# One program block instead of two, and the first gate product ahead of the last value products

## The chip, the cores and the metric

The kernel runs on one core of a Trainium2 chip. The metric is the device time of one launch in microseconds (us); less is better. The core has five engines that run their own programs and meet at semaphores: TensorE (PE in the profile), VectorE (DVE), ScalarE (ACT), GpSimd (POOL) and SyncE (SP), which here issues nearly all DMA transfers.

## The reference, cut to what matters

A pre-norm transformer layer over x of 4 batches, 512 tokens, width 512, in fp32. Attention has 32 query heads in 8 key/value groups (4 heads share a group, head width 16), rotary positions and a causal mask; the feed-forward width is 1376.

```python
x = x + attn(layernorm(x), Wq, Wk, Wv, Wo)    # softmax(mask(q k^T / 4)) v, then @ Wo
x = x + ffn(layernorm(x), Wg, Wu, Wd)         # (silu(x Wg^T) * (x Wu^T)) @ Wd^T
```

## The kernel before

There are two stages, `phase_1` and `phase_2`, and each opens a block of programs of its own, one program for each engine. At the end of a block all engines meet at a barrier and jump; then the next block begins. Tiles and PSUM banks of the first stage are given back at its end, and those of the second lie over them.

**Stage one, attention.** A batch is an iteration of 32 slots: 8 groups `g` with 4 slots `i` each. In a slot TensorE makes transposed scores of group n (`scores_t`, tile `ps_t`), the scores of group n+2 that give the row maximum (`scores`, `ps_s`), and pieces of dense work: the projections of the next batch, and in the last iteration the output projection of batch 0. ScalarE takes the exponential of `ps_t` into `probs`, GpSimd zeroes what the causal mask forbids (`mask_probs`, semaphore `probs_masked`), and TensorE multiplies `probs` with the values (`weighted_v`, tile `ps_o`, four chunks c of 512, 384, 256 and 128 columns). Chunks 0 and 1 of a group run in its own last slot, chunks 2 and 3 in the second slot of the next group. There is one `ps_o`: chunk 0 of a group waits until the group before it has been copied out (`o_evacuated`). That copy is ScalarE's, except for groups in the table `LAST_O` of the last iteration, which VectorE copies (`last_output`). The copy is stored to DRAM by SP.

The rotated queries and keys are split into parts: GpSimd makes a remainder (`rest_op`), ScalarE copies the high bits in the slots of `LO_SLOT` (`rotated_top`, tile `r_top`), and SP stores the parts one slot later (`store_rotated`). In the next slot with i = 0 SP loads the rows of a later group (`stage_rows`), and with i = 1 the transposed maximum (`stage_max`, `q_rows<-m_t`), which the next group's scores wait for. SP works its list in order.

In the last iteration the second stage's first operands are made too: xt of batch 0 from the transposed x (`last_xt`, VectorE, slots of `LAST_XT`: a cast to `xt_hi`, and the difference `xt_lo`), and the first three tiles of the gate and up weights (`split_ffn`). With these, TensorE has all that the first products of stage two read.

**Stage two, feed-forward.** For each batch, f runs over 11 tiles of the width. TensorE makes the gate and the up product (12 matmuls of 512 columns each, in four PSUM banks used in turn), for f from 3 to 6 the output projection of the next batch (`project_out`), and the down product of tile f-1 (12 matmuls into `ps_y`). Weights are fp32 as two parts: SP loads the raw tile (`load_ffn`), ScalarE casts it to the high part (`split_ffn_hi`), VectorE subtracts (`split_ffn_lo`). In the first batch ScalarE's program begins with the high parts of the down weights 0 and 1, and only then follows the first silu:

```python
            split_ffn_hi(0)
            split_ffn_hi(1)
            iteration(0, True)
```

SP's program of stage two begins with down tile 0, waits until the last group's output has landed in DRAM (`last_o_stored`), loads the last batch's softmax sums, then down tiles 1 and 2, the attention output for the next batch's first projection, and the weights of tile 3, 4 and so on:

```python
            load_ffn(0)
            sp.wait_ge(to.last_o_stored, DMA)
            sp.dma_start(sums, row_sums(d, B - 1)).then_inc(sums_loaded, DMA)
            load_ffn(1)
            load_ffn(2)
```

In iteration f of the first batch ScalarE and VectorE split tile f+2 before they scale and split the attention output (`scale_ctx`, `ctx_high`, `ctx_low`) that the projection at f+1 reads.

Of the kernel before, what the change touches and what calls it, by code (L numbers as in the profile page):

```python
# [1 line left out]

# [3 lines left out]
F32 = mybir.dt.float32  # L6
# [3 lines left out]
ALU = mybir.AluOpType  # L10
# [80 lines left out]
LO_SLOT = {7: 0, 13: 1, 16: 2, 23: 3, 27: 4}  # L91
# [3 lines left out]
LAST_O = {26: 5, 30: 6}  # L95
# [42 lines left out]
def rope_step(b, s):  # L138

    return PRE_STEPS + (KEY_STEPS + 2 * PAIR_STEPS) * (b - 1) + s + 1  # L140

# [117 lines left out]
def phase_1(nc, d, to):  # L259
    with ExitStack() as ctx:  # L260
# [6 lines left out]
        def sem(name):  # L267
            return ctx.enter_context(nc.semaphore(name))
# [91 lines left out]
        ffn_hi_ready = sem("first_ffn_hi_ready")  # L360
        sums_loaded = sem("sums_loaded")
# [50 lines left out]
        block = ctx.enter_context(nc.Block())  # L412


        @block.sync
        def _(sp):
# [146 lines left out]
        @block.gpsimd  # L563
        def _(pool):
# [155 lines left out]
        @block.scalar  # L720
        def _(act):
# [98 lines left out]
            def iteration(b, has_next):  # L820
                done = pieces_at(UNITS_IN[b])[1]
                for slot in range(TT * NKV):
# [4 lines left out]
                    if i == PV_EVACUATE and n >= 1 and (has_next or slot not in LAST_O):  # L827
# [53 lines left out]
        @block.vector  # L881
        def _(dve):
# [72 lines left out]
            def split_ffn(c):  # L955

                dve.wait_ge(ffn_hi_ready, c + 1)
                nc.vector.tensor_tensor(w_lo[:, c], w_lo[:, c].bitcast(F32), w_hi[:, c].bitcast(F32), ALU.subtract)
# [151 lines left out]
        @block.tensor  # L1110
        def _(pe):
# [114 lines left out]
            def weighted_v(b, g, c):  # L1226
                n = NKV * b + g
                pe.wait_ge(probs_masked, TT * n + c + 1)
                if c == 0:
                    if positive(n):  # L1230
                        pe.wait_ge(o_evacuated, n)
                    if g == 0:
                        pe.wait_ge(v_ready, b + 1)
                for j in range(GROUP):
                    mm = nc.tensor.matmul(ps_o[32 * j:32 * j + 2 * DH, P * c:T], v_ones[:, c, g % NKV, :],  # L1235
                                          probs[:, g % 2, j, CHUNK_AT[c]:CHUNK_AT[c + 1]],
                                          start=(c == 0), stop=(c == TT - 1))
                if c == TT - 1:
                    mm.then_inc(pv_done, 1)

            def iteration(b, has_next):
                pieces = pieces_at(UNITS_IN[b])[0]
                for slot in range(TT * NKV):
                    g, i = slot // TT, slot % TT
                    n = NKV * b + g
                    for j in range(GROUP):
# [3 lines left out]
                        if (i, j) in PV_AT:  # L1250
                            after, chunks = PV_AT[i, j]
                            for c in chunks if n + after >= 0 else ():
                                weighted_v(b, g + after, c)
# [32 lines left out]


# [21 lines left out]
def phase_2(nc, d, to):  # L1309
    with ExitStack() as ctx:  # L1310
# [3 lines left out]
        def sem(name):  # L1314
            return ctx.enter_context(nc.semaphore(name))
# [57 lines left out]
        block = ctx.enter_context(nc.Block())  # L1373

        @block.sync
        def _(sp):
# [40 lines left out]

            load_ffn(0)
# [21 lines left out]
        @block.gpsimd  # L1440
        def _(pool):
# [3 lines left out]
        @block.scalar  # L1445
        def _(act):
# [40 lines left out]

            split_ffn_hi(0)
# [6 lines left out]
        @block.vector  # L1495
        def _(dve):
# [74 lines left out]
        @block.tensor  # L1571
        def _(pe):
# [48 lines left out]
            def down(b, f):  # L1621
# [4 lines left out]
                if f == 0 and (not isinstance(b, int) or b > 0):  # L1626
# [8 lines left out]
            def iteration(b, has_next):  # L1635
# [4 lines left out]
                for f in range(FT):  # L1640
# [3 lines left out]
                    for name, weights, ready in (("gate", gate_weights, gate_ready), ("up", up_weights, up_ready)):  # L1644
# [3 lines left out]
                                       lambda q, c: xt[q][:, c, :], KC).then_inc(ready, 1)  # L1648
                    if has_next and 0 <= f - WO_SLOT < TT:
# [7 lines left out]

            iteration(0, True)
# [3 lines left out]


def build(nc, d):
# [51 lines left out]
```

## Time and profile before

| | |
|---|---|
| three runs | 770.94, 773.19, 773.08 us; median 773.08 |
| the profiled execution | 772.49 us, its span 770.8 us, 1.69 us around it |
| PE busy | 737.8 us, 96% of the span |
| DVE, ACT, POOL busy | 445.2, 333.8 and 241.9 us |
| granted TensorE clock | 0.989 of full speed |
| stage one | from 0 to 369.6 us of the span |
| stage two | from 369.6 us to the end |

The profile is of one execution. "Busy" adds up instructions of an engine; a time in brackets is what the engine stood idle ahead of an instruction, and the arrow names what ended it. Where the engine named had long been done, something else ended the wait.

### The profile page before, as it was taken

What the parts mean: (1) busy time and instruction counts of PE and PEld (TensorE: products, weight loads), DVE (VectorE), ACT (ScalarE), POOL (GpSimd) and SP (SyncE); (2) the same over time, 40 slices, a digit from 0 to 9 for tenths busy, and PEclk for the clock granted to TensorE, in tenths of its full rate; (3) what the DMA queues carried; (4) which work ended last, traced back from release to release, by engine and by line L of the source; (5) the groups of instructions that cost most, each with busy time, mean ns of one, the idle gap of its engine ahead of it and who ended that gap; (6) DMA issues with size and microseconds to landing.
All of it is one profiled execution on the core that took longest, in us unless ns stands there. A gap on an engine that the chain in (4) does not pass through costs nothing.

```text
span 770.8 us, 12186 instructions
## 1 busy us (share of the span) xinstructions
PE 737.8 (96%) x4149; PEld 502.4 (65%) x4164; DVE 445.2 (58%) x1136; ACT 333.8 (43%) x646; POOL 241.9 (31%) x467
## 2 busy tenths in 40 slices
PE   5889999999999999998999999999999999999998
PEld 4645444554444543443788888888888888788886
DVE  6897789888987889997355443234232333231212
ACT  4337678767976778667343222111121111111111
POOL 4257885688658774556000000000000000000000
PEclk9869999999999999999999999999999999999999
DMA  7337587234434455530592103211014020030001
GB/s 272 98 108 250 182 280 239 67 87 125 119 96 130 142 179 151 160 99 29 174 310 72 42 14 118 88 59 51 14 48 142 27 82 27 0 110 1 1 0 55
DMA packets 74759, 81.86 MB, mean 106 GB/s; under 512 B 8864, under 2 KB 58528, under 8 KB 74496
## 3 DMA queue, kind: packets, MB, share of 16 engines
q1 hardware_dynamic: 73408, 79.98, 32.7%
q10 hardware_dynamic: 1296, 1.18, 0.5%
q8 instruction: 30, 0.49, 0.3%
q14 instruction: 25, 0.20, 0.1%
HBM read 57.02 MB, written 33.36 MB: 117 GB/s over the span
## 4 chain that ended last, share of the span: by engine, by line
PE 51%; DVE 0%; issue 0%; DVEq 0%
PE bank L1578 35%; PE ps_y L1630 15%; PE bank L1617 1%; DVE x_in L1560 0%; DVEq L1559 0%
## 5 line engine op out<-in xcount | busy, mean ns | idle before, releaser
L929 DVE CUSTOM_DVE_ANT_0 ps_s<-ps_s,mask_row 128x512 f32<-128x512 f32 (+1 forms) x360 | 192.1, 583 | 36.6 <-PE ps_s L1188 34.0
L792 ACT ACTIVATE probs<-ps_t 128x512 f32<-128x512 f32 (+1 forms) x352 | 178.2, 560 | 68.6 <-PE ps_t L1222 68.3
L1535 DVE TENSOR_TENSOR h<-h,bank 128x512 f32<-128x512 f32 (+1 forms) x44 | 30.2, 687 | 212.8 <-PE bank L1578 211.6
L1188 PE MATMUL ps_s<-k_rows,q_rows 96*128 96x256 bf16 (+3 forms) x512 | 141.0, 309 | 5.7 <-DVE m_raw L929 2.9
L1222 PE MATMUL ps_t<-q_rows,k_rows 98*128 98x512 bf16 (+1 forms) x352 | 126.9, 364 | 4.4 <-DMA q_rows<-m_t 2.4
L240 POOL TENSOR_TENSOR var_eps<-mean_var,eps 128x1 f32<-128x1 f32 x16 | 3.0, 189 | 281.7 <-DVE mean_var L235 281.7
L1473 ACT ACTIVATE h<-bank 128x512 f32<-128x512 f32 (+1 forms) x44 | 26.3, 597 | 145.2 <-PE bank L1578 145.2
L1235 PE MATMUL ps_o<-probs,v_ones 128*32 128x512 f32 (+3 forms) x1024 | 82.0, 438 | 3.4 <-POOL probs L693 1.1
L693 POOL TENSOR_SCALAR_AFFINE_SELECT probs<-probs 128x512 f32<-128x512 f32 x128 | 83.4, 652 | 0.0
L1479 ACT CAST h_hi<-h 128x512 fp32r<-128x512 f32 (+1 forms) x44 | 27.3, 620 | 126.5 <-DVE h L1535 126.5
L1188 PEld LDWEIGHTS ps_s<-k_rows,q_rows 96*128 96x128 bf16 x512 | 48.2, 100 | 47.8 <-DVE m_raw L929 22.3
L1630 PE MATMUL ps_y<-wd_hi,h_hi 128*128 128x512 f32 (+1 forms) x176 | 68.8, 391 | 0.0
L1222 PEld LDWEIGHTS ps_t<-q_rows,k_rows 98*128 98x128 bf16 x352 | 34.2, 98 | 53.1 <-issue 18.3
L1630 PE MATMUL ps_y<-wd_lo,h_hi 128*128 128x512 f32 (+1 forms) x176 | 68.5, 389 | 0.0
L1630 PE MATMUL ps_y<-wd_hi,h_lo 128*128 128x512 f32 (+1 forms) x176 | 68.5, 389 | 0.0
L1235 PEld LDWEIGHTS ps_o<-probs,v_ones 128*32 128x32 f32 x1024 | 27.2, 109 | 43.3 <-issue 30.4
L691 POOL TENSOR_TENSOR carrier<-half 128x1 f32<-128x1 f32 x128 | 26.8, 209 | 89.9 <-ACT probs L792 89.8
L929 DVE DVE_READ_ACCUMULATOR2_ANT m_raw<- 128x1 f32 x360 | 50.3, 140 | 0.0
L1578 PE MATMUL bank<-xt_hi,wg_hi 128*128 128x512 f32 (+1 forms) x128 | 50.0, 390 | 0.0
L1578 PE MATMUL bank<-xt_hi,wg_lo 128*128 128x512 f32 (+1 forms) x128 | 49.9, 390 | 0.0
L1578 PE MATMUL bank<-xt_hi,wu_lo 128*128 128x512 f32 (+1 forms) x128 | 49.9, 390 | 0.0
L1578 PE MATMUL bank<-xt_lo,wu_hi 128*128 128x512 f32 (+1 forms) x128 | 49.9, 390 | 0.0
(167 smaller groups left out, 1366.1 us busy)
## 6 DMA issues: line engine op xcount, KB each, us to landing
scratch_o<-o_sb SPq DMA_DIRECT2D x31, 256.0 KB, 2.4
q_rows<-scratch_q_parts SPq DMA_DIRECT2D x32, 192.0 KB
x_in<-in_x SPq DMA_DIRECT2D x16, 256.0 KB, 4.0
q_rows<-scratch_q_parts SPq DMA_DIRECT2D x32, 128.0 KB
o_in<-scratch_o SPq DMA_DIRECT2D x64, 64.0 KB
inverse<-scratch_inverse SPq DMA_DIRECT2D x64, 64.0 KB
x_res<-in_x SPq DMA_DIRECT2D x16, 256.0 KB, 2.7
out<-x_in SPq DMA_DIRECT2D x16, 256.0 KB, 2.1
```

Source lines behind the costliest of these rows:

```text
L691: nc.gpsimd.tensor_tensor(carrier[:, g % 2, c:c + 1], half[:, 0:1], half[:, 0:1], ALU.add)
L693: nc.gpsimd.affine_select(out=diagonal, in_=diagonal, compare_op=ALU.is_ge, fill=0.0, base=0, pattern=[[0, GROUP], [1, P]], channel_multip ...
L792: nc.scalar.activation(probs[:, g % 2, heads * u:heads * (u + 1), CHUNK_AT[c]:CHUNK_AT[c + 1]], ps_t[:, pos % S_BANKS, 0:heads * CHUNK_N[c ...
L929: taken = nc.vector.tensor_tensor_reduce(out=head, in0=head, in1=mask_row[:, T - width:T], scale=1.0, scalar=LOWEST, op0=ALU.add, op1=ALU. ...
L1188: mm = nc.tensor.matmul(bank[:, place], q_rows[r][0:ROWS, j, P * q:P * (q + 1)], k_rows[r][0:ROWS, 0:width], start=(place == 0), stop=(mas ...
L1222: nc.tensor.matmul(ps_t[:, pos % S_BANKS, 0:heads * width], k_rows[r][:, P * c:P * (c + 1)], q_rows[r][:, heads * u:heads * (u + 1), P * c:T],
L1235: mm = nc.tensor.matmul(ps_o[32 * j:32 * j + 2 * DH, P * c:T], v_ones[:, c, g % NKV, :], probs[:, g % 2, j, CHUNK_AT[c]:CHUNK_AT[c + 1]], ...
L1473: nc.scalar.activation(h[0:m, r], bank[units["gate", f] % BANKS][0:m, :], ACT.Silu).then_inc(silu_done, 1)
L1479: nc.scalar.copy(h_parts[0][0:m, r], h[0:m, r]).then_inc(h_hi_ready, 1)
L1535: nc.vector.tensor_tensor(h[0:m, r], h[0:m, r], bank[units["up", f] % BANKS][0:m, :], ALU.mult).then_inc(h_ready, 1)
L1578: mm = nc.tensor.matmul(out, weights(w, c), moving(m, c), start=(c == 0 and n == 0), stop=(c == chunks - 1 and n == 2))
L1630: mm = nc.tensor.matmul(ps_y[:, t], h_parts[w][0:m, r, P * t:P * (t + 1)], wd[p][0:m, f, :], start=(f == 0 and k == 0), stop=(f == FT - 1 ...
```

## The change

Four things are done.

1. The two stages return their programs instead of opening blocks, and one block calls the first and then the second. The barrier between them is gone. In its place single waits stand: SP and ScalarE wait for the copy of the last group's output (`handed_over`) at the start of stage two, TensorE waits for it ahead of its first down product, and ahead of its first gate product it waits for `xt_lo` and for the split gate weights (`first_tiles_ready`).
2. TensorE makes the first gate product before chunks 2 and 3 of the last group's value products (`last_values`).
3. `LAST_O` moves VectorE's copy of group 6 of the last batch from slot 30 to slot 29, ahead of the third `last_xt`.
4. `LO_SLOT` moves three of the five copies of high bits of each batch ahead: from slots 16, 23 and 27 to 14, 22 and 26.

```diff
-LO_SLOT = {7: 0, 13: 1, 16: 2, 23: 3, 27: 4}
+LO_SLOT = {7: 0, 13: 1, 14: 2, 22: 3, 26: 4}
-LAST_O = {26: 5, 30: 6}
+LAST_O = {26: 5, 29: 6}
...
-                if not has_next:
-                    for c in (2, 3):
-                        weighted_v(b, NKV - 1, c)
-
...
+        def last_values(pe):
+
+            for c in (2, 3):
+                weighted_v(pe, B - 1, NKV - 1, c)
...
+        def handed_over(engine):
+
+            engine.wait_ge(o_evacuated, GROUPS)
+
+        def first_tiles_ready(pe):
+
+            pe.wait_ge(dense_evacuated, LAST_UNIT0 + TT + KC)
+            pe.wait_ge(ffn_split, KC)
...
+            attention.handed_over(sp)
             load_ffn(0)
             sp.wait_ge(to.last_o_stored, DMA)
...
+            attention.handed_over(act)
             split_ffn_hi(0)
             split_ffn_hi(1)
...
-                if f == 0 and (not isinstance(b, int) or b > 0):
+                if f == 0 and isinstance(b, int) and b == 0:
+                    attention.handed_over(pe)
+                elif f == 0:
                     pe.wait_ge(y_evacuated, TT * b)
...
+                        if first and (name, f) == ("gate", 0):
+                            attention.last_values(pe)
...
+            attention.first_tiles_ready(pe)
             iteration(0, True)
...
-        phase_1(nc, d, handover)
-        phase_2(nc, d, handover)
+        attention = phase_1(nc, d, handover, ctx)
+        feed_forward = phase_2(nc, d, handover, ctx, attention)
+        block = ctx.enter_context(nc.Block())
...
+        @block.tensor
+        def _(pe):
+            attention.tensor(pe)
+            feed_forward.tensor(pe)
```

TensorE between the stages, before: the value products of the last group, the two jumps, and the first gate product (`bank`). The names in brackets are the semaphores that an instruction waits for.

```order
L1235 MATMUL ps_o<-probs,v_ones 32x384 x3
L1235 MATMUL ps_o<-probs,v_ones 32x256 [waits probs_masked]
L1235 MATMUL ps_o<-probs,v_ones 32x256 x3
L1235 MATMUL ps_o<-probs,v_ones 32x128 [waits probs_masked]
L1235 MATMUL ps_o<-probs,v_ones 32x128 x3
L260 UNCONDITIONAL_BRANCH
L1571 UNCONDITIONAL_BRANCH [waits barrier_Pool_Activation_PE_DVE_SP_release]
L1578 MATMUL bank<-xt_hi,w_hi 128x512
```

The same place now, from the last chunk-1 product to the first of the up product; of the twelve matmuls of the gate product the first and the last two are shown.

```order
L1132 MATMUL ps_o<-probs,v_ones 32x384 x3
L1600 MATMUL bank<-xt_hi,w_hi 128x512 [waits first_ffn_split,dense_evacuated]
...
L1600 MATMUL bank<-xt_lo,w_hi 128x512
L1600 MATMUL bank<-xt_hi,w_lo 128x512
L1132 MATMUL ps_o<-probs,v_ones 32x256 [waits probs_masked]
L1132 MATMUL ps_o<-probs,v_ones 32x256 x3
L1132 MATMUL ps_o<-probs,v_ones 32x128 [waits probs_masked]
L1132 MATMUL ps_o<-probs,v_ones 32x128 x3
L1600 MATMUL bank<-xt_hi,w_hi 128x512
```

The eight matmuls of chunks 2 and 3 now stand behind the gate product, and with them everything that waits for the last group's output.

VectorE's last work of stage one, before: `COPY o_sb` is group 6, `COPY o_in` group 7, each `CAST` with the `TENSOR_TENSOR` behind it one `last_xt`.

```order
L958 TENSOR_TENSOR w_lo<-w_lo,w_hi 128x768 [waits first_ffn_hi_ready]
L979 CAST xt_hi<-ps_s 128x512 [waits dense_ready]
L901 TENSOR_TENSOR xt_lo<-ps_s,xt_hi 128x512 [waits xt_hi_ready]
L986 COPY o_sb<-ps_o 128x512 [waits o_stored0,pv_done]
L979 CAST xt_hi<-ps_s 128x512 [waits dense_ready]
L901 TENSOR_TENSOR xt_lo<-ps_s,xt_hi 128x512 [waits xt_hi_ready]
L986 COPY o_in<-ps_o 128x512 [waits pv_done]
```

And now.

```order
L970 TENSOR_TENSOR w_lo<-w_lo,w_hi 128x768 [waits first_ffn_hi_ready]
L999 COPY o_sb<-ps_o 128x512 [waits o_stored0,pv_done]
L992 CAST xt_hi<-ps_s 128x512 [waits dense_ready]
L913 TENSOR_TENSOR xt_lo<-ps_s,xt_hi 128x512 [waits xt_hi_ready]
L992 CAST xt_hi<-ps_s 128x512 [waits dense_ready]
L913 TENSOR_TENSOR xt_lo<-ps_s,xt_hi 128x512 [waits xt_hi_ready]
L999 COPY o_in<-ps_o 128x512 [waits pv_done]
```

Group 6's copy stands ahead of two `last_xt` instead of one.

SP in a batch of stage one around slots 14 to 17, before: `r_top` and `r_low` are `store_rotated`, `k_rows` and `q_rows<-scratch_q_parts` are `stage_rows`, `q_rows<-m_t` is `stage_max`.

```order
L434 DMA scratch_wu_raw<-in_wu 16x11008 x2
L452 DMA k_rows<-scratch_k_parts 48x1x512
L455 DMA q_rows<-scratch_q_parts 48x4x512
L452 DMA k_rows<-scratch_k_parts 32x1x512
L455 DMA q_rows<-scratch_q_parts 32x4x512
L452 DMA k_rows<-scratch_k_parts 16x512
L455 DMA q_rows<-scratch_q_parts 16x4x512
L409 DMA scratch_q_parts<-r_top 16x8x512 x2
L409 DMA scratch_q_parts<-r_low 16x8x512
L465 DMA q_rows<-m_t 2x16x128
```

And now.

```order
L449 DMA scratch_wu_raw<-in_wu 16x11008
L426 DMA scratch_q_parts<-r_top 16x8x512 x2
L426 DMA scratch_q_parts<-r_low 16x8x512
L449 DMA scratch_wu_raw<-in_wu 16x11008
L467 DMA k_rows<-scratch_k_parts 48x1x512
L470 DMA q_rows<-scratch_q_parts 48x4x512
L467 DMA k_rows<-scratch_k_parts 32x1x512
L470 DMA q_rows<-scratch_q_parts 32x4x512
L467 DMA k_rows<-scratch_k_parts 16x512
L470 DMA q_rows<-scratch_q_parts 16x4x512
L480 DMA q_rows<-m_t 2x16x128
```

The three stores moved ahead of the six row loads; ahead of `q_rows<-m_t` stand the same transfers as before.

## Rows read from the trace of the kernel before

**Rows 1.** Waits of TensorE from 369 to 771 us: total, times, longest.

```profile
PE bank L1578 <- PEq L260: 1.9, 1, 1.9
```

**Rows 2.** Timeline of TensorE between the stages: start, duration, instruction, idle before.

```profile
361.69 0.62 PE L1235 MATMUL ps_o<-probs,v_ones 128*32 128x256 f32 x12
...
363.88 0.38 PE L1222 MATMUL ps_t<-q_rows,k_rows 98*128 98x512 bf16 x1
365.38 2.36 PE L1235 MATMUL ps_o<-probs,v_ones 128*32 128x512 f32 x32 [1.11 <-POOL probs L693]
369.60 0.47 PE L1578 MATMUL bank<-xt_hi,w_hi 128*128 128x512 f32 x1 [1.86 <-PEq L260]
```

**Rows 3.** Timeline of VectorE there.

```profile
361.31 0.95 DVE L958 TENSOR_TENSOR w_lo<-w_lo,w_hi 128x768 fp32r<-128x768 f32 x1
...
363.94 0.69 DVE L901 TENSOR_TENSOR xt_lo<-ps_s,xt_hi 128x512 fp32r<-128x512 f32 x1
364.55 0.68 DVE L986 COPY o_sb<-ps_o 128x512 f32<-128x512 f32 x1
365.14 0.68 DVE L979 CAST xt_hi<-ps_s 128x512 fp32r<-128x512 f32 x1
365.86 0.69 DVE L901 TENSOR_TENSOR xt_lo<-ps_s,xt_hi 128x512 fp32r<-128x512 f32 x1
367.79 0.69 DVE L986 COPY o_in<-ps_o 128x512 f32<-128x512 f32 x1 [1.24 <-PE ps_o L1235]
```

**Rows 4.** Timeline of GpSimd there: the mask of chunk 1.

```profile
363.70 0.63 POOL L693 TENSOR_SCALAR_AFFINE_SELECT probs<-probs 128x512 f32<-128x512 f32 x1
```

**Rows 5.** Timeline of SP's queue behind the last copy.

```profile
368.51 0.33 SPq L471 DMA_DIRECT2D scratch_o<-o_in  x1
...
370.50 0.62 SPq L1420 DMA_DIRECT2D x_res<-scratch_o  x1
371.18 1.05 SPq L1393 DMA_DIRECT2D wd_lo<-scratch_wd_raw  x2
```

**Rows 6.** Timelines of ScalarE, VectorE and TensorE: down tile 1 to the first down product.

```profile
374.00 0.62 ACT L1452 CAST wd_hi<-wd_lo 128x512 fp32r<-128x512 f32 x1 [1.30 <-DMA wd_lo<-scratch_wd_raw]
374.63 1.28 ACT L1473 ACT_TABLE_LOAD   x1
...
377.94 0.69 DVE L1540 TENSOR_TENSOR h_lo<-h,h_hi 128x512 fp32r<-128x512 f32 x1 [0.69 <-ACT h_hi L1479]
...
380.57 0.39 PE L1630 MATMUL ps_y<-wd_hi,h_hi 128*128 128x512 f32 x1
```

**Rows 7.** The same engines and SP: weight tile 4 to the first projection.

```profile
387.13 0.51 SPq L1393 DMA_DIRECT2D wd_lo<-scratch_wd_raw  x1
...
391.65 0.62 ACT L1451 CAST wg_hi<-wg_lo 128x512 fp32r<-128x512 f32 x1 [1.31 <-DMA wd_lo<-scratch_wd_raw]
...
395.49 0.69 DVE L218 TENSOR_TENSOR ctx_lo<-o_in,ctx_hi 128x512 fp32r<-128x512 f32 x1 [0.69 <-ACT ctx_hi L213]
...
396.89 0.39 PE L1578 MATMUL bank<-wo_hi,ctx_hi 128*128 128x512 f32 x1
```

**Rows 8.** Stage one: SP's stores and maximum at slot 17, and TensorE's wait.

```profile
100.28 1.22 SPq L409 DMA_DIRECT2D scratch_q_parts<-r_top  x2
...
102.94 0.68 SPq L465 DMA_DIRECT2D q_rows<-m_t  x1
...
106.10 0.39 PE L1222 MATMUL ps_t<-q_rows,k_rows 98*128 98x512 bf16 x1 [0.66 <-DMA q_rows<-m_t]
```

**Rows 9.** TensorE's longest wait after its start, and clock by stretch: us, busy (instructions), clock, DMA share, GB/s.

```profile
33.58 1.12 PE L1149 MATMUL ps_t<-ident,v_t 128*128 128x128 f32 x4 [2.64 <-ACT v_t L759]
...
33.00:36.00 3.00, 1.74 (x7) 0.55 0.28 88
...
42.00:45.00 3.00, 3.00 (x14) 0.50 0.49 130
...
364.00:370.00 6.00, 3.03 (x36) 1.00 0.22 86
```

More of the change, by code:

```diff
@@ L1 @@
 from contextlib import ExitStack
+from dataclasses import dataclass
+from typing import Callable
 import concourse.bass as bass
@@ L140, in rope_step @@
     return PRE_STEPS + (KEY_STEPS + 2 * PAIR_STEPS) * (b - 1) + s + 1
+@dataclass
+class Programs:
+    sync: Callable
+    gpsimd: Callable
+    scalar: Callable
+    vector: Callable
+    tensor: Callable
+    last_values: Callable = None
+    handed_over: Callable = None
+    first_tiles_ready: Callable = None
 class Handover:
@@ L267, in sem @@
         def sem(name):
[L268 removed]
+            return sems.enter_context(nc.semaphore(name))
         ident = to.ident
@@ L826, in iteration @@
                         max_evacuate(n + 1)
-                    if i == PV_EVACUATE and n >= 1 and (has_next or slot not in LAST_O):
+                    if i == PV_EVACUATE and n >= 1 and (has_next or g - 1 not in LAST_O.values()):
                         o_evacuate(b, g - 1)
@@ L1107, in _, with weighted_v, tensor_engine @@
             last_output(NKV - 1)
-        @block.tensor
-        def _(pe):
+        def weighted_v(pe, b, g, c):
+            n = NKV * b + g
+            pe.wait_ge(probs_masked, TT * n + c + 1)
+            if c == 0:
+                if positive(n):
+                    pe.wait_ge(o_evacuated, n)
+                if g == 0:
+                    pe.wait_ge(v_ready, b + 1)
+            for j in range(GROUP):
+                mm = nc.tensor.matmul(ps_o[32 * j:32 * j + 2 * DH, P * c:T], v_ones[:, c, g % NKV, :],
+                                      probs[:, g % 2, j, CHUNK_AT[c]:CHUNK_AT[c + 1]],
+                                      start=(c == 0), stop=(c == TT - 1))
+            if c == TT - 1:
+                mm.then_inc(pv_done, 1)
+        def last_values(pe):
+            for c in (2, 3):
+                weighted_v(pe, B - 1, NKV - 1, c)
+        def tensor_engine(pe):
             PRODUCTS = ((0, 0), (0, 1), (1, 0))
@@ L1224, in scores_t @@
                                  start=True, stop=True).then_inc(scores_t_ready, 1)
[L1226 to L1239, printed above, removed]
             def iteration(b, has_next):
@@ L1252, in iteration @@
                             for c in chunks if n + after >= 0 else ():
-                                weighted_v(b, g + after, c)
+                                weighted_v(pe, b, g + after, c)
                         for place, kind, k, piece in pieces.get((slot, j), ()):
@@ L1306, with phase_2 @@
 RING_LAST = ring_units(False)
-def phase_2(nc, d, to):
+def phase_2(nc, d, to, sems, attention):
     with ExitStack() as ctx:
@@ L1666, in build, with _ @@
         handover = Handover(nc, ctx)
-        phase_1(nc, d, handover)
-        phase_2(nc, d, handover)
+        attention = phase_1(nc, d, handover, ctx)
+        feed_forward = phase_2(nc, d, handover, ctx, attention)
+        block = ctx.enter_context(nc.Block())
+        @block.sync
+        def _(sp):
+            attention.sync(sp)
+            feed_forward.sync(sp)
+        @block.gpsimd
+        def _(pool):
+            attention.gpsimd(pool)
+            feed_forward.gpsimd(pool)
+        @block.scalar
+        def _(act):
+            attention.scalar(act)
+            feed_forward.scalar(act)
+        @block.vector
+        def _(dve):
+            attention.vector(dve)
+            feed_forward.vector(dve)
+        @block.tensor
+        def _(pe):
+            attention.tensor(pe)
+            feed_forward.tensor(pe)
 def rope_tables():
```

40 lines of the change are left out of this document (17 added, 23 removed).

## The prediction

> **What bounds the kernel now.** I read the page's busy times first: TensorE is busy for 96% of the span. Then its waits by stretch. In stage two the view has a single entry [rows 1], the wait that ends at 369.60: once started, TensorE runs to the end with no wait on another engine, so an operand that comes earlier brings nothing there, and one that comes later than TensorE needs it costs its full lateness. Time can only be won ahead of 369.60. The timeline there [rows 2] has two holes. After the last transposed scores (363.88) the value products start at 365.38, after 1.11 us idle, and after they end (365.38 + 2.36 = 367.74) the first gate product starts at 369.60, after 1.86 us.
>
> Who ends them? The first is put down to GpSimd's mask, but the mask of chunk 1 was done at 363.70 + 0.63 = 364.33 [rows 4], and that of chunk 0 before it. The other condition of chunk 0 is group 6's copy, which VectorE ended at 364.55 + 0.68 = 365.23 [rows 3], about 0.1 before the products. So the copy was the wait. It could have run earlier: its value products ended at 361.69 + 0.62 = 362.31 [rows 2] and VectorE's weight split at 361.31 + 0.95 = 362.26 [rows 3]. The second hole is the last copy (367.79 to 368.48), SP's store and the barrier. The gate product itself needs none of this: `xt_lo` was done at 365.86 + 0.69 = 366.55 [rows 3].
>
> **The change, part by part: TensorE up to the up product.** With the copy at 362.4, chunks 0 and 1 can start behind the last scores, at about 364.2. How long do they take? Matmuls of 1280 columns in all four chunks took 2.36 us, so the 896 columns of the first two take 1.65 and the other two 0.7, to which I give 0.15 for the changes of shape: until 365.85, and 0.85. On VectorE the last cast moves into the slot that the copy held, 364.55, and the last difference follows 365.86 - 365.14 = 0.72 later, at 365.27, and ends at 365.96. The gate product therefore starts at 366.1, held by `xt_lo` by some 0.2. It takes 12 steps of (380.57 - 369.60)/48 = 0.2285 us [rows 2, 6], 2.74, and with 0.1 at its start the values of chunks 2 and 3 begin at 368.95 and end at 369.8; their masks were ready by 366.2. The up product starts at 369.75. Before it started at 369.60 + 2.74 = 372.35. **TensorE is 2.6 us ahead here.** The barrier and the jumps are part of the 1.86 us, and what replaces them is covered by the gate product.
>
> **What hangs on the last value products.** The same move makes the last group's output later in absolute time: copy at 369.85 instead of 367.79, **2.06 us later**. Behind that copy stands SP's whole list: store at 370.57 (368.51 before), sums load when the store has landed, 370.50 - 368.51 = 1.99 later, at 372.56, and only then down tile 1, at 373.24 (371.18) [rows 5]. The 0.7 us saved between the store and down tile 0 by the missing barrier does not help, since the list waits for the store. ScalarE casts tile 1 ahead of its first silu, so it starts at 374.00 + 2.06 = 376.06 [rows 6]; table load, silu, product, cast and difference follow as before, and `h_lo` is done at 377.94 + 0.69 + 2.06 = 380.69. TensorE wants it at 369.75 + 36 steps = 377.95. **It waits 2.8 us and starts the down product at 380.75, against 380.57 before.** The lead is gone, and 0.2 more. The cover that hid this chain was 380.57 - 378.63 = 1.94 us; 2.06 later and 2.6 sooner needed is more than it has.
>
> I weigh one rule here. On this chain the row has the table load at 1.28 us, with the silu 0.02 behind it [rows 6]. The Trainium skill (ScalarE: Activation LUTs, What ACT_TABLE_LOAD costs) gives about 1.28 us and a drain of 1.38 on top; the trace has the first and shows no drain. By the page `h_lo` would come 1.4 later and the total below would be +1.6 instead of +1.45; the measured row decides.
>
> What is late next? SP issued from 370.50 to beyond 387.13 without a wait that showed, so the later transfers shift by 2.06 too. Weight tile 4 (last issue 387.13) is what ScalarE waited for at 391.65; from there the splits and the scaling run one after another to `ctx_lo`, done at 395.49 + 0.69 = 396.18 [rows 7]. TensorE started the projection at 396.89: cover 0.7. Now `ctx_lo` is done at 398.24 and TensorE, by then 0.2 late, arrives at 397.07. **It waits another 1.25 us and starts at 398.33, 1.45 after its old time.** The tiles behind have more room: their steps on TensorE are 10.9 us apart and ScalarE waited for no further tile in the trace. The rest of the kernel keeps the 1.45.
>
> **Stage one.** The copies of high bits are moved, not added. ScalarE does the same 1.05 us in a slot where the next exponential is needed by TensorE two products later; I cost it at nothing, with 0.3 as bound for each of three places in three batches where it might not be covered, 0.9 at most if a third of them miss. The gain would be in the waits for `q_rows<-m_t`, such as 0.66 at 106.10. But SP is the queue in front of it, issuing back to back (stores 100.28, maximum 102.94) [rows 8], and the stores stand ahead of the maximum now as before, so it goes out at the same time. Bounds from below: all four such waits, 2.4 us in total. I take 0, being nearest to the queue's order, and keep -0.7 to +0.9. Six row loads go out 1.9 us later at slot 16 (100.2 to 102.0), and are read at 105.6; the maximum, issued later still at 102.94, landed by 106.1, so they just make it.
>
> **Sum.** -2.6 + 2.8 + 1.25 = +1.45 us, on the profiled execution's own 772.49 us: 773.9, which I give as 774.0 with a little for stage one. The median of the three runs is 0.6 above the profiled execution, so against it this is a change of 0.1 to 0.2%, inside the 0.3% (2.3 us) that a measurement of this kernel tells from no change.
>
> **Rivals.**
> - *No late tile* (16%). If down tile 1 lands so much sooner that `h_lo` is ready at 378, and tile 4 likewise, the 2.6 us stay: 769.9, faster. For it: in the old trace the two loads were issued 1.6 us apart beside the sums, now down tile 0 is out of the way longer. Against: tile 1 took 374.00 - 371.18 = 2.8 us, and the store alone 1.99, so nearly three would have to vanish.
> - *Only the first wait* (12%). If tile 4 isn't 2 us later, since SP's list has slack I don't see, the sum is +0.2: 772.7, no change.
> - *The clock falls* (15%). This one ends slower. After a wait of 2.64 us at 33.58 the granted clock was 0.55 in the next stretch and still 0.50 at 42 to 45, that is 1.2 GHz; with 1.11 and 1.86 us idle at 364 to 370 it stayed 1.00 [rows 9]. A wait of 2.8 us is of the first kind. At half clock each us costs 0.5; the first 1.25 us lost are free, as they only fill the second wait. So the total is 0.2 + L for a loss L above 1.25, and the kernel is slower by 0.3% once the low clock lasts over 4.2 us; up to 12 us would be 778.7, and 7 us, between, 776.2. Against: TensorE is dense from there on, which it wasn't at 33. The Trainium skill (TensorE: Matmul & The Clock Gate, What's actually happening) says that the low clock is the default and activity releases it, which leaves both open.
> - *Stage one moves after all* (7%): 1 in 7 of it faster, the others split between no change and slower, 772 to 777.
>
> **How the numbers follow.** The forecast has 50%, with a range of its own of 773.0 to 775.2 (0.9 for stage one, and 0.5 for landing times each way). Faster is the first rival and a bit of the last, 0.17; no change the forecast, the second rival and half of the last, 0.65; slower the clock and the rest, 0.18. The range runs from the first rival's 769.8 to 776.3, which leaves out the longer half of the clock's case and little else.
>
> **What the next profile would show.** Right: no idle ahead of the last group's first value products; the gate product at 366.1 with the values behind it; the last copy at 369.85; SP's sums load 2.0 us behind its store; a wait of about 2.8 us ahead of the first `ps_y` product, on VectorE's `h_lo`, and one of 1.2 ahead of the first `wo` product, on `ctx_lo`; TensorE's total of waits in stage two near 4 us. Wrong: no wait at `ps_y` (first rival), a clock below 1.00 behind 378 (third), or the last scores of stage one more than 1 us away from 363.88 (fourth).

## The result and the profile after

The changed kernel takes 775.74 us (median of 8 executions) against 773.13 for the kernel before; the ratio is 1.0049, with a 95% interval of 1.0033 to 1.0066. So it is slower, by 0.3 to 0.7%. Measured again in a later series it was 775.68 against 772.28, ratio 1.0036 [1.0021, 1.0052]. I had forecast no change (774.0). The ratio is not the quotient of the two medians, which is 1.0034 in the first series and 1.0044 in the second.

The profiled execution was the slowest of the eight, 778.65 us with a span of 776.9. Its busy times are those of before plus 3.7 us of TensorE, on matmuls that are the same in number:

```profile
PE 741.5 (95%) x4149; PEld 503.9 (65%) x4164; DVE 445.1 (57%) x1136; ACT 334.2 (43%) x646; POOL 242.5 (31%) x467
```

More busy time on the same work suggests a lower clock. First the timeline of TensorE between the stages, the counterpart of [rows 2]:

```profile
367.99 0.38 PE L1254 MATMUL ps_t<-q_rows,k_rows 98*128 98x512 bf16 x1
368.30 1.71 PE L1132 MATMUL ps_o<-probs,v_ones 128*32 128x512 f32 x16
370.11 0.50 PE L1600 MATMUL bank<-xt_hi,w_hi 128*128 128x512 f32 x1
...
373.06 0.86 PE L1132 MATMUL ps_o<-probs,v_ones 128*32 128x256 f32 x16
373.85 0.50 PE L1600 MATMUL bank<-xt_hi,w_hi 128*128 128x512 f32 x1
...
384.97 0.47 PE L1654 MATMUL ps_y<-wd_hi,h_hi 128*128 128x512 f32 x1 [2.62 <-issue]
```

The last scores stand 4.11 us later than before (367.99 against 363.88). From there the order does what it says: both holes are gone, the gate product starts 2.12 us behind the scores (5.72 before), the up product at 5.86 (8.47 before). Then comes the wait ahead of the first down product, 2.62 us. The chain that it waits for begins in SP's queue, in its timeline (counterpart of [rows 5]):

```profile
374.70 0.33 SPq L486 DMA_DIRECT2D scratch_o<-o_in  x1
375.36 0.33 SPq L1417 DMA_DIRECT2D wd_lo<-scratch_wd_raw  x1
376.70 0.63 SPq L1445 DMA_DIRECT2D x_res<-scratch_o  x1
377.38 1.06 SPq L1417 DMA_DIRECT2D wd_lo<-scratch_wd_raw  x2
```

and goes on in those of ScalarE and VectorE (counterparts of [rows 6]):

```profile
380.24 0.62 ACT L1475 CAST wd_hi<-wd_lo 128x512 fp32r<-128x512 f32 x1 [1.67 <-DMA wd_lo<-scratch_wd_raw]
380.88 1.28 ACT L1496 ACT_TABLE_LOAD   x1
382.18 0.60 ACT L1496 ACTIVATE h<-bank 128x512 f32<-128x512 f32 x1
...
384.18 0.69 DVE L1563 TENSOR_TENSOR h_lo<-h,h_hi 128x512 fp32r<-128x512 f32 x1 [0.68 <-ACT h_hi L1502]
```

Each row stands 4.13 to 4.18 us behind the time forecast for it (store 370.57, sums 372.56, tile 1 373.24, cast 376.06), which is the lateness of stage one and nothing else: this chain was forecast to a tenth. The table load again took 1.28 us with the silu 0.02 behind it. The Trainium skill (ScalarE: Activation LUTs, What ACT_TABLE_LOAD costs) has a drain on top; this trace doesn't show one either.

What I had only as a rival is the clock behind the wait, here by windows (columns: window, length, busy and instructions, granted clock, DMA share, GB/s):

```profile
382.00:385.00 3.00, 0.38 (x3) 1.00 0.47 119
385.00:388.00 3.00, 3.00 (x9) 0.60 0.74 186
388.00:392.00 4.00, 4.00 (x17) 0.87 0.76 230
```

A mean of 0.60 is the half clock (1.2 GHz, 0.50) for 80% of 3 us, and 0.87 for 26% of 4 us: together 3.4 us, of which half is lost. No wait stands ahead of the first projection. Where do the 4.1 us of stage one come from? Most of it shows in one place. TensorE's timeline has a wait there:

```profile
127.94 0.39 PE L1254 MATMUL ps_t<-q_rows,k_rows 98*128 98x512 bf16 x1 [1.99 <-DMA q_rows<-m_t]
```

and the windows around it show the clock:

```profile
124.00:128.00 4.00, 1.86 (x19) 1.00 0.86 266
128.00:132.00 4.00, 4.00 (x17) 0.70 0.86 289
132.00:136.00 4.00, 3.94 (x36) 0.87 0.25 75
```

Again a wait of 2 us, and half clock behind it. Before, TensorE had no wait here. The wait is for the transposed maximum of slot 25, so I looked at SP's queue, first in the kernel before:

```profile
113.92 1.19 SPq L434 DMA_DIRECT2D scratch_wd_raw<-in_wd  x2
116.41 1.22 SPq L409 DMA_DIRECT2D scratch_q_parts<-r_top  x2
...
118.35 0.77 SPq L452 DMA_DIRECT2D k_rows<-scratch_k_parts  x1
...
121.75 0.67 SPq L465 DMA_DIRECT2D q_rows<-m_t  x1
```

and in the changed one:

```profile
114.89 0.57 SPq L449 DMA_DIRECT2D scratch_wd_raw<-in_wd  x1
116.89 1.22 SPq L426 DMA_DIRECT2D scratch_q_parts<-r_top  x2
...
118.80 1.39 SPq L449 DMA_DIRECT2D scratch_wd_raw<-in_wd  x1
120.24 0.77 SPq L467 DMA_DIRECT2D k_rows<-scratch_k_parts  x1
...
123.62 0.67 SPq L480 DMA_DIRECT2D q_rows<-m_t  x1
```

Before, SP issued two weight copies and then stood idle from 115.11 until the rotated parts were ready at 116.41. Now the stores stand ahead of the second copy: SP waits about as long (1.43 us against 1.30), and the copy, 1.39 us of issue, falls behind the stores. The maximum goes out 1.87 us later, of which 0.95 is the kernel's general lateness by then (110.80 against 109.85 for the maximum before it) and 0.92 is new. That can't be all of a wait of 1.99 us: TensorE now starts 4.32 us behind the issue of the maximum, where before it started 3.32 behind it (at 125.07) without a wait. So the maximum also landed later behind its own issue. What that comes from is taken up behind the experiments on the queue.

### The profile page after: what moved, and what is told of

Its sections match the earlier page's. It is cut to its first block, busy times and chain, and to the rows that moved or that the text cites. A ratio compares the mean times of both kernels' runs of the same rounds, so it can differ in the third digit from the quotient of the medians.

```text
span 776.9 us, 12176 instructions
## 1 busy us (share of the span) xinstructions
PE 741.5 (95%) x4149; PEld 503.9 (65%) x4164; DVE 445.1 (57%) x1136; ACT 334.2 (43%) x646; POOL 242.5 (31%) x467
## 4 chain that ended last, share of the span: by engine, by line
PE 81%; DVE 7%; POOL 4%; ACT 3%; DMA 2%; issue 2%; ACTq 0%; SPq 0%; POOLq 0%; DVEq 0%
PE bank L1600 35%; PE ps_y L1654 15%; PE ps_t L1254 7%; PE ps_o L1132 7%; PE ps_s L1220 6%; PE ps_d L1172 6%; DVE ps_s L941 2%; DMA q_rows<-m_t 2%; ACT probs L805 2%; PE ps_d L1193 1%; POOL rot L609 1%; POOL turned L609 1%; PE bank L1639 1%; POOL rot L613 1%; POOL probs L707 1%
```

## The experiments

"Scores to end" is the time from the start of the last transposed scores to the end of the span; it holds the handover and stage two, and nothing of stage one. Before it was 770.8 - 363.88 = 406.9. Each value is of one profiled execution. All ratios are to the kernel before, executed in turn with it.

**The LO_SLOT table alone** (kernel before, new table).

```diff
-LO_SLOT = {7: 0, 13: 1, 16: 2, 23: 3, 27: 4}
+LO_SLOT = {7: 0, 13: 1, 14: 2, 22: 3, 26: 4}
```

> The kernel before with the changed LO_SLOT alone; the two blocks stay. Two theories. A (two places): in the changed kernel's profile stage one ended 4.1 us later, and its first loss stands at 124 to 128, where SP stores the high bits ahead of a weight copy that used to fill SP's idle time, the transposed maximum is issued 0.9 later than its surroundings, TensorE waits 1.99 us and its clock is below 1.00 for some 10 us. Then this kernel is slower than before by 1 to 4 us, with that wait of 1.5 to 2 us near 127. B (handover only): that was one execution's accident, and this kernel is within 0.5 us of before in the median, with a wait below 0.7 there.

774.58 against 772.57 us, ratio 1.0023 [1.0007, 1.0039]. A wait of 2.24 us at 127.17, with the clock at 0.50 from 130 to 132. So stage one's loss comes with this table alone, and needs nothing of the rest of the change.

**The changed kernel with the old LO_SLOT.**

> The changed kernel with LO_SLOT of before: one block, first gate product ahead of the last value products, earlier copy of group 6. A: stage one as before (the last transposed scores end within 1 us of 363.9), up product 2.6 us earlier than before, a wait of 2.6 us ahead of the first ps_y product, then some 3 us at half clock that cost 1.5 to 2 us, no wait or one under 1.2 ahead of the first projection; in all +1.5 to +2.2 us against before. B: nearly the whole slowdown of the changed kernel, +2.3 to +3 us.

773.71 against 772.57, ratio 1.0015 [0.9999, 1.0030]. The last scores at 363.59, a wait of 2.65 ahead of the down product, the clock 0.50 at 382 to 384, scores to end 408.9: 2.0 more than the profile of before. The median says 1.2. The difference of the two numbers became clear only later (below, the clock).

**All value products ahead of the gate product** (single block kept, old LO_SLOT).

```diff
-                        if first and (name, f) == ("gate", 0):
-                            attention.last_values(pe)
...
+            attention.last_values(pe)
             attention.first_tiles_ready(pe)
             iteration(0, True)
```

> As the one with the old LO_SLOT, but all four chunks of the last value products stand ahead of the gate product; the single block stays. Theory A (the order costs, the barrier was the gain): values end near 366.5, the gate product starts at 366.6 instead of 369.6, the last copy ends near 367.4 (368.48 before), so the chain to h_lo ends near 377.6 and TensorE wants it at 377.6: a wait under 0.3 at ps_y, the clock stays at 1.00; ahead of the first projection a wait of about 1 us, since ctx_lo is only 1.05 earlier. In all -1.5 to -2.5 us against before. Rival C (the gate product ahead is what gains, the masks of chunks 2 and 3 hold TensorE without it): gate product not before 367.5, and a total within 1 us of before.

770.22 against 772.57, ratio 0.9975 [0.9961, 0.9989]: faster than before; scores to end 405.0. TensorE's timeline:

```profile
362.57 0.38 PE L1254 MATMUL ps_t<-q_rows,k_rows 98*128 98x512 bf16 x1
362.88 2.40 PE L1132 MATMUL ps_o<-probs,v_ones 128*32 128x512 f32 x32
365.21 0.50 PE L1600 MATMUL bank<-xt_hi,w_hi 128*128 128x512 f32 x1
...
393.58 0.50 PE L1600 MATMUL bank<-wo_hi,ctx_hi 128*128 128x512 f32 x1 [0.68 <-DVE ctx_lo L233]
```

The masks of chunks 2 and 3 do not hold TensorE: all four chunks run in 2.40 us without a gap. The gate product starts 2.64 us behind the scores, 0.5 later than with the gate product first, and the up product, twelve steps on at 368.06, at 5.49 against 5.86: earlier. Moving the gate product ahead filled no time that was still empty, and it held the last copy back by a whole product. Rival C falls.

**SP issues down tiles 1 and 2 ahead of its wait for the last store** (gate product first, old LO_SLOT).

```diff
             load_ffn(0)
+            load_ffn(1)
+            load_ffn(2)
             sp.wait_ge(to.last_o_stored, DMA)
             sp.dma_start(sums, row_sums(d, B - 1)).then_inc(sums_loaded, DMA)
-            load_ffn(1)
-            load_ffn(2)
```

> As the one with the old LO_SLOT (gate product first), but SP issues down tiles 1 and 2 ahead of its wait for the last store. Theory A: the cast of tile 1 follows that of tile 0 at once, h_lo is 1.6 us earlier, so the wait ahead of ps_y is 1.0 to 1.2 us instead of 2.6 and the clock stays at 1.00; then a wait of 1.5 to 2.9 us ahead of the first projection, as weight tile 4 and what follows it come at most 1.1 earlier; in all +0.3 to +1.5 us against before. If instead the tiles were not what h_lo waits for, the wait at ps_y stays at 2.6 and the time that of the kernel with the old LO_SLOT.

773.38 against 772.57, ratio 1.0006 [0.9994, 1.0018]. TensorE's waits of stage two, in its timeline:

```profile
379.67 0.47 PE L1654 MATMUL ps_y<-wd_hi,h_hi 128*128 128x512 f32 x1 [1.05 <-issue]
398.82 0.50 PE L1600 MATMUL bank<-wo_hi,ctx_hi 128*128 128x512 f32 x1 [2.59 <-DVE ctx_lo L233]
```

and the windows behind the second (the granted clock stands behind the count of instructions):

```profile
398.00:400.00 2.00, 1.18 (x5) 0.93 1.12 363
400.00:402.00 2.00, 2.00 (x6) 0.50 1.13 359
```

The first wait fell from 2.6 to 1.05, as worked out, and the second operand in line took it over: 2.59 us ahead of the projection, and the half clock came there instead. Scores to end is 410.1, 1.2 more than with the old LO_SLOT alone, but this execution was the slowest of its twelve. By the medians the two kernels are alike (773.38 and 773.71). This shows both chains of the forecast, and that mending this one alone gives little or nothing.

**Both repairs**: the tiles ahead, and ctx ahead of the split of tile f+2, on ScalarE and in the same way on VectorE.

```diff
+                    if has_next and 0 <= f - WO_SLOT + 1 < TT:
+                        ctx_hi(b + 1, f - WO_SLOT + 1)
                     if first and f + 2 < FT:
                         split_ffn_hi(f + 2)
-                    if has_next and 0 <= f - WO_SLOT + 1 < TT:
-                        ctx_hi(b + 1, f - WO_SLOT + 1)
```

With the gate product first:

> The same two repairs (tiles ahead of the store's wait, ctx ahead of the split) with the gate product first, as in the changed kernel, and the old LO_SLOT. If tile 4 ahead of ctx was the cause of the 2.6 us ahead of the first projection: that wait is gone, the 1.0 us ahead of ps_y stays (nothing repairs it), the clock stays at 1.00, -1.3 to -1.6 us against before, so 1.5 us behind the values-first kernel with the same repairs. Rival: a wait of over 1 us ahead of the projection stays, and the time is within 0.5 us of before.

771.78 against 773.48, ratio 0.9980 [0.9959, 1.0001]. The wait ahead of the projection is gone, 1.15 us ahead of the down product is left, the clock stays; scores to end 405.6. With the value products first:

> A kernel meant to beat both: old LO_SLOT, one block, all value products ahead of the gate product, SP issues down tiles 1 and 2 ahead of its wait for the last store, and ScalarE and VectorE make the attention output's parts ahead of the split of tile f+2. From the values-first kernel's trace: the gate product starts 3.1 us sooner behind the last scores than before, and its only wait in stage two was 0.7 ahead of the first projection, which the new order of ctx and split should take away. If lateness of ctx_lo came from tile 4 standing ahead of it: no wait of TensorE in stage two over 0.2 us, clock 1.00, -3.0 to -3.3 us against before. Rival: ctx_lo is held by its own loads, and the 0.7 stays; -2.4 us.

769.73 against 773.48, ratio 0.9955 [0.9931, 0.9978]. Stage two has no wait left; scores to end 403.7, 3.2 below before. A second series, beside the changed kernel:

> The kernel with all value products first, down tiles ahead of the store's wait and ctx ahead of the split, once more beside the changed one: no wait in stage two, clock 1.00 there, -2.5 to -3.5 us against before and some 5 to 6 us ahead of the changed kernel.

768.77 against 772.28, ratio 0.9954 [0.9937, 0.9972]. The counterpart of [rows 2], from that profile:

```profile
364.31 0.38 PE L1254 MATMUL ps_t<-q_rows,k_rows 98*128 98x512 bf16 x1
364.62 2.40 PE L1132 MATMUL ps_o<-probs,v_ones 128*32 128x512 f32 x32
366.95 0.50 PE L1600 MATMUL bank<-xt_hi,w_hi 128*128 128x512 f32 x1
...
377.96 0.39 PE L1654 MATMUL ps_y<-wd_hi,h_hi 128*128 128x512 f32 x1
...
394.28 0.39 PE L1600 MATMUL bank<-wo_hi,ctx_hi 128*128 128x512 f32 x1
```

No brackets: nothing stands idle. This version beats both kernels, by 3.5 and 6.9 us.

**The single block alone** (values first, LO_SLOT and LAST_O of before).

> The single block alone: value products ahead of the gate product, LO_SLOT and LAST_O of before. The 1.1 us hole ahead of the last value products is back, and only the barrier's part of the other hole is won, so the gate product starts some 2.0 us sooner behind the last scores than before; the last copy stays where it was, so h_lo and ctx_lo come as late as before. Theory (only as much lead is kept as the tightest operand allows, 0.7 at ctx_lo): waits of under 0.3 at ps_y and about 1.3 ahead of the first projection, -0.5 to -0.9 us in all. Rival (what is won ahead of the gate product stays won): -2.0 us.

771.49 against 773.48, ratio 0.9987 [0.9964, 1.0009], too wide to decide by time. The profile decides: the gate product starts 3.78 behind the scores instead of 5.72, so 1.94 are won there, and scores to end is 406.2, so 0.7 are kept. The rival that all of it stays won falls by this profile; the interval of the ratio (-2.8 to +0.7 us) would still hold it. The wait ahead of the projection was 0.68, not 1.3: TensorE came there 0.4 later than reckoned (31.50 us behind the scores, where 33.01 - 1.94 = 31.07 was), and `ctx_lo` some 0.2 sooner than before.

**The weight copy issued ahead of the stores** (kernel before, new LO_SLOT), in slots 15 and 23 of the first iteration.

```diff
+                    if not positive(b) and slot in (15, 23):
+                        copy_raw(2 * g + i - 2)
                     if has_next and slot - 1 in LO_SLOT:
                         store_rotated(sp, b + 1, LO_SLOT[slot - 1])
...
-                    if not positive(b) and i >= 2 and g < 6:
+                    if not positive(b) and i >= 2 and g < 6 and slot not in (15, 23):
                         copy_raw(2 * g + i - 2)
```

> The kernel before with the changed LO_SLOT, and in slots 15 and 23 of the first iteration the weight copy is issued ahead of the stores, so that it fills SP's wait for them again. Theory A (queue order: the copy of 1.4 us behind the stores delays the maximum): the wait of 2 us near 127 and the half clock behind it are gone (a wait under 0.7 there, clock 1.00), and the time is within 0.7 us of before. Rival (ScalarE's copy of high bits in the earlier slots is what costs): the wait and +1.5 to +2 us stay.

775.22 against 773.48, ratio 1.0022 [1.0006, 1.0039]. The two readings disagree: no wait over 0.35 us from 112 to 135, but the median was as far off as with the table alone. By the time, theory A had fallen; so I took the entries apart. The same profile has the rest of the answer: ahead of two other maxima TensorE waited 1.17 us (at 106.75) and 1.04 us (at 267.7), where before it was 0.66 and nothing.

**Entry 23 to 22 alone**, twice, and **the other two entries alone.**

> The kernel before with one entry of LO_SLOT changed, 23 to 22. Theory A (this entry alone puts the stores ahead of the last weight copy, which delays the maximum near 127): the wait of about 2 us near 127 and the half clock behind it are here, and most of what LO_SLOT costs, +1 to +2 us. Rival: it is shared by the other two entries, +0.5 us or less and a wait under 1 us near 127.

> The kernel before with LO_SLOT 23 changed to 22, a second time. +1 to +3 us whatever the cause; between 124 and 128 a wait of 0.7 to 2.3 us.

> The kernel before with the other two entries changed, 16 to 14 and 27 to 26. Theory A: no wait over 1 us near 127; only the small waits for the maximum near 106 and 269 grow, by 0.4 and 0.5 to 1.0, as in the two profiles with the changed table: +0.3 to +1.2 us. Rival (the weight copy was not the cause, since issuing it first left the time as it was): +1.5 us or more.

Entry 22: 774.61 against 772.28, ratio 1.0033 [1.0016, 1.0049], and 773.67 against 771.90, 1.0016 [1.0001, 1.0030]. The other two: 773.32 against 772.28, 1.0012 [0.9996, 1.0028]. The wait near 126 was 0.71 us in the first profile; TensorE's timeline of the second shows:

```profile
127.00 0.39 PE L1222 MATMUL ps_t<-q_rows,k_rows 98*128 98x512 bf16 x1 [2.12 <-DMA q_rows<-m_t]
```

and its window behind that wait:

```profile
128.00:132.00 4.00, 3.66 (x35) 1.00 0.96 325
```

So the wait varies from one execution to the next, and here no half clock followed it.

**Queue order or ScalarE's copy?** Entry 22 with the weight copy first, and entry 22 for ScalarE only, with SP's stores left in slot 24 by a table of their own:

```diff
-LO_SLOT = {7: 0, 13: 1, 16: 2, 23: 3, 27: 4}
+LO_SLOT = {7: 0, 13: 1, 16: 2, 22: 3, 27: 4}
+STORE_SLOT = {8: 0, 14: 1, 17: 2, 24: 3, 28: 4}
...
-                    if has_next and slot - 1 in LO_SLOT:
-                        store_rotated(sp, b + 1, LO_SLOT[slot - 1])
+                    if has_next and slot in STORE_SLOT:
+                        store_rotated(sp, b + 1, STORE_SLOT[slot])
```

> The kernel before with LO_SLOT 23 changed to 22, and the weight copy of slot 23 issued ahead of the stores. Queue order as the cause: within 0.8 us of before, no wait over 0.5 us between 124 and 128. ScalarE as the cause: +1.5 us or more, as with the entry alone.

> The kernel before with ScalarE's copy of high bits in slot 22 instead of 23, and SP's stores left in slot 24. Queue order as the cause: within 0.8 us of before. ScalarE as the cause: +1.5 us or more.

772.40 against 771.90, ratio 0.9995 [0.9979, 1.0011], and 770.94 against 771.90, 0.9986 [0.9970, 1.0001]. Neither costs anything that shows, and neither profile has a wait of TensorE over 0.7 us between 45 and 280. For this entry ScalarE is cleared, and the queue order is the cause of what it costs; the profiles carry this more than the times, whose intervals still overlap with that of the entry alone (1.0001 to 1.0030).

With the other two entries in, the kernel with the copy first still measured +1.7 us; the two entries alone measured +0.9 with an interval that includes that. The profiles say where it goes. Ahead of the maximum near 106 us TensorE waited 0.99 us on average in the five profiles with these entries (0.78 to 1.17) and 0.53 in the thirteen without them (0.36 to 0.91); ahead of the one near 267 it was 0.83 (0.53 to 1.14) against 0.09 (nothing in ten, 0.74 at most). Together that is 1.2 us. So the other two entries are the likely rest; no run shows what in their place makes these waits.

**The changed kernel, and its version with the old LO_SLOT, once more.**

> The changed kernel once more, unchanged, for a second profile and more executions. If its first profile was typical: waits of about 2 us near 127 and 2.6 us ahead of the first ps_y product, granted clock 0.50 behind both, no wait ahead of the first projection, +2 to +4 us against before. If the stage-one wait was an accident of one execution, it is below 1 us here and the kernel is within 1.5 us of before.

> The changed kernel with the old LO_SLOT, a second time: a wait of 2.6 to 2.8 us ahead of the first ps_y product. Behind it the clock is 0.50 for some 3.4 us (2 of the 3 profiles with this wait so far) or stays at 1.00 (1 of 3), and the stretch from the last scores to the end is 408.9 us with the fall, about 407.5 to 408 without. +0 to +2.3 us against before.

The changed kernel: ratio 1.0036 as above, waits of 1.12 near 125 and 2.79 ahead of the down product, neither followed by a lower clock, as the windows of its second profile show:

```profile
124.00:128.00 4.00, 3.19 (x21) 1.00 0.92 325
...
378.00:382.00 4.00, 1.21 (x6) 1.00 0.52 120
382.00:385.00 3.00, 3.00 (x15) 1.00 0.84 242
```

Its profiled execution took 773.94, the fastest of its series. With the clock up the second wait of the forecast is there in TensorE's timeline, but small:

```profile
398.26 0.50 PE L1600 MATMUL bank<-wo_hi,ctx_hi 128*128 128x512 f32 x1 [0.23 <-DVE ctx_lo L233]
```

The old LO_SLOT: 774.32 against 771.90, ratio 1.0025 [1.0011, 1.0039], a wait of 2.67, half clock behind it, scores to end 408.8.

**How the queue order costs.** This last profile has SP's old order, and it happens to issue the row loads and the maximum just as late as the changed kernel did. From the timelines of SP's queue and of TensorE:

```profile
113.84 1.19 SPq L449 DMA_DIRECT2D scratch_wd_raw<-in_wd  x2
...
119.20 0.77 SPq L467 DMA_DIRECT2D k_rows<-scratch_k_parts  x1
...
122.59 0.68 SPq L480 DMA_DIRECT2D q_rows<-m_t  x1
...
125.14 0.39 PE L1254 MATMUL ps_t<-q_rows,k_rows 98*128 98x512 bf16 x1 [0.23 <-DMA q_rows<-m_t]
```

TensorE was ready at 125.14 - 0.23 = 124.91, so the maximum was issued 2.32 us ahead of that and the first row load 5.71 ahead. In the changed kernel it was 2.33 and 5.71 (ready at 127.94 - 1.99 = 125.95). The issue times are alike, and the waits are 0.23 and 1.99. So the issue of the maximum is not what makes the wait; its landing is. In the five profiles with the stores ahead of the second weight copy TensorE started 3.05 to 4.45 us behind the issue of the maximum. In the thirteen with both copies ahead of the stores it started 2.2 to 3.7 us behind it, with a wait of 0.48 at most, and in five of these the maximum was issued as late as 2.20 to 2.41 us ahead of the need.

What differs is the weight copy, 688 KB, which took 5.1 to 6.6 us from issue to landing by the DMA view (for the pair of copies that is the median). Reckoned with that, it landed behind the issue of the maximum in all five, and before it in the thirteen. That the two transfers hold each other up is my reading of this; no run changes the copy's size or takes it away. The issue itself isn't fixed either: SP took 1.39 to 1.52 us to issue the moved copy in three profiles and 0.6 in two.

**The clock behind the handover.** Eight profiles have the old handover (the kernel before and seven with stage-one edits only), all with the idle 1.86 or 1.87 us ahead of the gate product. In five of them, the clock fell behind it; these are windows of the one with the weight copies of slots 15 and 23 first:

```profile
370.00:372.00 2.00, 1.34 (x5) 0.86 0.52 181
372.00:374.00 2.00, 2.00 (x7) 0.50 0.42 132
374.00:376.00 2.00, 2.00 (x8) 0.79 0.75 276
```

| handover | profiles | half clock behind it | scores to end, us |
|---|---|---|---|
| as before | 3 | no | 406.8 to 406.9 |
| as before | 5 | yes | 408.5 |
| changed (either LO_SLOT) | 1 | no | 407.9 |
| changed (either LO_SLOT) | 3 | yes | 408.8 to 408.9 |
| changed, with the tiles ahead | 1 | yes, behind the later wait | 410.1 |
| changed, both repairs | 1 | no | 405.6 |
| single block alone | 1 | no | 406.2 |
| values first | 1 | no | 405.0 |
| values first, both repairs | 2 | no | 403.7 |

## Why the prediction was wrong

**TensorE to the up product: right.** 2.12 us from scores to gate product (2.2 forecast), 5.86 to the up product (5.87 forecast).

**The chain to the down product: right.** A wait of 2.62, 2.79, 2.65 and 2.67 us in the four profiles with this handover, 2.8 forecast.

**The wait ahead of the projection: mis-sized.** 1.25 forecast. Where the clock had fallen there was none, as the rival said that the first of the lost time is free there; where it stayed up it was 0.23. The term "the later transfers shift by 2.06 too" was too large for that profile: `ctx_lo` ended 33.9 us behind the scores against 32.3 before, 1.6 later (in the four profiles it was 1.4 to 2.1); and TensorE came 0.6 later than forecast.

**The clock behind the wait: I gave it 15%.** It fell in three of four profiles, for some 3.4 us, where I had put the price for the sign at 4.2 us and more. The rival's own formula, 0.2 and half of the fall, gives +1.9 for it, and 408.9 is 2.0 more than in the profile of before. By itself that does not carry the handover over the bound.

**What the sum was made against: not seen.** The step that took the idle 1.86 us of [rows 2] as safe, because the clock "stayed 1.00" in [rows 9], rested on one execution, and on a window that ends at 370, 0.4 us behind the idle time. In that execution it did stay up further on; over all it fell in five of eight. With a fall the old handover takes 408.5, and a kernel that loses 1.6 us to the clock half of the time is a slower base than the trace that I subtracted from. Weighted by these counts the handover went from 407.9 to 408.6, +0.7; the two series gave +1.2 [-0.1, 2.3] and +1.9 [0.8, 3.0] us. My +1.45 is near that, partly by luck: the too large second wait stood in for the clock.

**Stage one: the step that failed.** I costed the moved copies of high bits at 0: the same transfers stand ahead of the maximum, "so it goes out at the same time". My bound of +0.9 was for ScalarE's copies. The table costs 1.8 us [0.5, 3.0] and moves the whole past the bound. That the same transfers stand ahead of the maximum was true, and how late it was issued did not decide. The stores moved past a weight copy, so the copy started later, and behind that order the maximum landed later: in the five profiles with it TensorE's wait was 0.71 to 2.24 us, in four of them 1.12 or more; in the profiles of the other kernels no wait there reached 0.5. I had also read from slot 17, [rows 8], that SP issues back to back, and carried it to slot 24, where it isn't so: there SP stands idle ahead of the stores until the parts are ready, and both weight copies used to be on their way by then. My working counted what is issued ahead of an instruction, and not which large transfer is still under way when it is issued.

Together: 1.8 from stage one and 1.2 to 1.9 from the handover are 3.0 to 3.7, and the two measurements of the changed kernel were 0.0049 and 0.0036 of 773, 3.8 and 2.8. The first rival (no late tile) has nothing in the traces for it. The second (only the first wait) is nearer to them than my sum in one point: the second wait was 0.23 us or none. But its time of 772.7 had neither the clock nor stage one.

## What to carry to other kernels

Work that is put ahead to fill a hole must be weighed against every operand that hangs on the work put behind it; once the hole was filled by an earlier copy and a missing barrier, the move bought nothing and cost a product's length. Sum up a lead as the smallest cover of the operands downstream: mending one chain moves the wait to the next, and only both repairs together, with the value products first, gave 3.5 us. In a queue that is worked in order ask of each moved entry which large transfer now starts behind it, and which small one behind that somebody waits for: that the same entries stand ahead of an issue doesn't say when its data is there. And before a difference of 2 us is worked out from one profile, find out whether a clock fall is part of that execution.

## What the runs showed of the hardware

After a short idle time of TensorE the clock falls or stays, and that decides on 1 to 2 us. From 60 us of the span on, the granted clock stayed at 1.00 behind all waits of 0.7 to 1.3 us. Behind 1.86 or 1.87 us it fell to 0.50 in five profiles of eight; behind 1.99 and 2.24 it fell and behind 2.12 it didn't; behind 2.6 to 2.8 it fell in four of five. Each of these falls lasted some 3.4 us. Early in the kernel it is harsher: behind the wait of 2.6 to 2.7 us near 34 us [rows 9] the clock was at 0.50 in all thirteen profiles that have this wait, and between 33 and 56 us it was low for 10 to 17 us in every profile. That idle time lowers the clock is as the Trainium skill has it (TensorE: Matmul & The Clock Gate, What's actually happening: the low clock is the default, and activity releases it); that the same idle time in the same kernel does it in one execution and not in the next is what I had not expected.

How much of the spread it makes can be read from the mean granted clock that is on record for every execution. The kernel before has 130 executions in four series. The nine with a clock of 0.987 took 775.3 us on average, the 45 with 0.989 took 773.3, the 36 with 0.993 took 771.2, and the six with 0.996 took 770.6. So most of the 6 us by which executions of one kernel differ goes with the clock.
